# A graph-attention kernel: the selection matrix of layers 0 and 1 made on ScalarE instead of VectorE

## What is computed

```
h   = (x @ W).reshape(N_NODES, HEADS, HEAD_DIM)          # 6250, 8, 32
el, er = sums of h * al and of h * ar over HEAD_DIM
e   = leaky_relu(el[src] + er[dst], 0.2)
ex  = exp(e - m[dst]);  a = ex / segment_sum(ex, dst)[dst]
out = segment_sum(h[src] * a, dst)                       # then bias, leaky_relu in layers 0 and 1
```

## Time and profile before

| | us |
|---|---|
| median of 3 runs | 7243.95 |
| lowest, highest | 7237.48, 7246.24 |
| the profiled execution's own time | 7240.56 |
| its span | 7238.9 |
| mean granted TensorE clock | 0.901 of full speed |

### The profile page before, as it was taken

One profiled execution on the slowest core, in us unless ns is written; L12 is line 12 of the kernel. 1 busy time (PEld: TensorE's weight loads), 2 busy tenths in 40 slices (PEclk: granted clock), 3 DMA queues, 4 the chain that ended last, 5 costly groups with the idle time before them and its releaser, 6 DMA issues.

```text
span 7238.9 us, 140830 instructions
## 1 busy us (share of the span) xinstructions
PE 5473.8 (76%) x35030; PEld 4419.5 (61%) x35031; DVE 4464.1 (62%) x9891; ACT 1582.9 (22%) x4669; POOL 4550.8 (63%) x4739
## 2 busy tenths in 40 slices
PE   4566677777776666666767665678888899999999
PEld 2445555565564454555555553456777778888888
DVE  5455566666665555666676765666666665655554
ACT  2000001111110000000000000013344444555554
POOL 0677777777765777777777757777655454444331
PEclk9788888888887788889898987789999999999999
DMA  4555555555544555555555444444433333222221
GB/s 168 175 142 146 146 148 149 150 152 148 144 140 116 142 142 145 144 144 146 147 148 144 139 118 135 140 133 129 118 110 104 93 95 87 83 84 80 73 73 41
DMA packets 386096, 916.18 MB, mean 127 GB/s; under 512 B 130561, under 2 KB 192777, under 8 KB 385930
## 3 DMA queue, kind: packets, MB, share of 16 engines
q0 software_dynamic: 227904, 681.63, 34.8%
q1 hardware_dynamic: 115530, 194.09, 7.9%
q10 hardware_dynamic: 42624, 40.02, 1.6%
HBM read 871.89 MB, written 43.49 MB: 126 GB/s over the span
## 4 chain that ended last, share of the span: by engine, by line
PE 28%; POOL 28%; issue 23%; DVE 8%; DVEq 7%; DMA 3%; ACTq 2%; ACT 2%; POOLq 1%; SPq 0%
POOL gat L411 27%; PE bank L1446 9%; PE bank L1373 9%; PE bank L1362 6%; DVEq L254 2%; DMA gat<-table,meta 2%; DVE msg L1116 2%; ACTq L254 1%; DVE selT L1088 1%; DVE sel L1124 1%; PE bank L1316 1%; DVE lg L1106 1%; ACT L501 1%; DVEq L1142 1%; DVEq L1107 0%
## 5 line engine op out<-in xcount | busy, mean ns | idle before, releaser
L411 POOL DMA_INDIRECT gat<-table,meta x4716 | 4537.5, 962 | 2538.3 <-issue 1366.3
L1446 PE MATMUL bank<-msg,sel 128*128 x10560 | 3174.8, 452 | 1347.2 <-DVE sel L1124 1330.3
L1446 PEld LDWEIGHTS bank<-msg,sel 128*128 128x128 f32 x10560 | 2183.5, 217 | 1810.8 <-issue 1436.9
L1116 DVE SCALAR_TENSOR_TENSOR msg<-bank,gat 128x1056 f32 x1320 | 1658.3, 1256 | 273.9 <-ACT bank L544 250.2
L544 ACT ACTIVATE bank<-lg 128x32 f32<-128x32 f32 x1320 | 262.8, 199 | 4620.5 <-DVE lg L1110 4485.3
L1124 DVE TENSOR_TENSOR sel<-iota_t,meta 128x512 f32<-128x512 f32 x1320 | 903.4, 684 | 93.9 <-PE bank L1446 90.1
L1106 DVE TENSOR_TENSOR lg<-gat,bank 128x64 f32<-128x64 f32 x880 | 193.3, 220 | 999.8 <-POOLq L418 759.3
L1373 PE MATMUL bank<-w,region 128*128 128x256 f32 x3136 | 758.5, 385 | 31.8 <-ACT region L501 31.6
L1362 PEld LDWEIGHTS bank<-xT,w 128*128 128x128 f32 x6272 | 750.5, 192 | 15.8
L1362 PE MATMUL bank<-xT,w 128*128 128x128 f32 x6272 | 759.6, 276 | 0.0
L1416 PEld LDWEIGHTS bank<-uvb,selT 128*128 128x128 bf16 x10584 | 391.3, 98 | 445.7 <-DVE selT L1088 252.8
(11 more groups left out here) (215 smaller groups left out, 2559.5 us busy)
## 6 DMA issues: line engine op xcount, KB each, us to landing
dstb<-dst_lists SPq DMA_DIRECT2D x297, 512.0 KB
gat<-table,meta POOLq DMA_INDIRECT x4716
table<-hrow ACTq DMA_DIRECT2D x98, 140.0 KB, 2.7
w<-in_W SPq DMA_DIRECT2D x2, 4096.0 KB
table<-hrow SPq DMA_DIRECT2D x49, 140.0 KB, 1.8
region<-xnT_d ACTq DMA_DIRECT2D x50, 128.0 KB
region<-qT_d ACTq DMA_DIRECT2D x50, 128.0 KB
res<-in_x SPq DMA_DIRECT2D x1, 6272.0 KB, 25.4
```

What stands on the lines that cost most here:

```text
L411: pool.indirect_dma_start(gat[:, r, c, :], None, table[l], bass.IndirectOffsetOnAxis(meta[:, m, c, 0:1].bitcast(U32), 0)).then_inc(s_done, 16)
L1116: dve_v.scalar_tensor_tensor(msg[:, bass.ds(n % 2, 1), :, :].rearrange("p a c (h d) -> p (a c) h d", h=H), ex_p.unsqueeze(3).to_broadcast( ...
L1446: last = pe.matmul(acc[:, 0:MSG], sel[:, c, :], msg[:, bass.ds(m % 2, 1), c, :].rearrange("p a m -> p (a m)"), start=opens and c == 0, sto ...
```

## The change

In layers 0 and 1 VectorE no longer makes `sel`. At the start of `logits` it subtracts the tile's base from the 512 destination numbers of the pass (`within`, 128x4, two buffers). ScalarE, behind its exponential of the pass, waits on `agg_done`, takes for each of the 4 blocks the absolute value of (bias - node number), drains, and turns the distances into 1 or 0 by max(0, 1 - distance); it reports on a semaphore of its own, `sel_ready`. VectorE's `messages` now signals `tile_first`, `slot_done` or `tile_last`, and TensorE waits on `sel_ready` ahead of those. `select` returns at once in these layers, and `iota_t` is written in layer 2 only. The rest of the diff merges some semaphores of the setup phase (`flags_ready`, `slots_ready` and their like into `step_ready` and `step_summed`), wait for wait; it is cut here.

```diff
+        within = sb("within", [P, 2, CH])
...
+        sel_ready = [sem(f"sel_ready{l}") for l in range(LAYERS - 1)]
...
                     act.wait_ge(logit_ready[l], n)
                     act.activation(ex_p, lg[:], ACT.Exp).then_inc(ex_ready[l], 1)
+                    if l + 1 < LAYERS:
+                        act.wait_ge(agg_done[l], n)
+                        for c in range(CH):
+                            act.activation(sel[:, c, :], iota, ACT.Abs,
+                                           bias=within[:, bass.ds(n % 2, 1), c:c + 1].rearrange("p a c -> p (a c)"), scale=-1.0)
+                        act.drain()
+                        act.activation(sel[:], sel[:], ACT.Relu, bias=ones[:, 0:1], scale=-1.0).then_inc(sel_ready[l], 1)
...
                 dve.sem_inc(agg_done[l], 1)
+                if l + 1 < LAYERS:
+                    dve.sem_inc(sel_ready[l], AHEAD)
...
+                    if l + 1 < LAYERS:
+                        dve_v.tensor_scalar(within[:, bass.ds(n % 2, 1), :].rearrange("p a c -> p (a c)"),
+                                            meta[:, bass.ds(g % LISTS, 1), :, 1:2].rearrange("p a c w -> p (a c w)"),
+                                            base[:, bass.ds(T, 1)], None, ALU.subtract)
                     dve.wait_ge(gathered[l], g)
...
-                    if opening:
+                    if opening and l + 1 == LAYERS:
                         dve_v.tensor_scalar(iota_t[:], iota, base[:, bass.ds(T, 1)], None, ALU.add)
...
-                def messages(g, n):
+                def messages(g, n, done):
...
-                    dve_v.scalar_tensor_tensor(
+                    product = dve_v.scalar_tensor_tensor(
...
+                    if l + 1 < LAYERS:
+                        product.then_inc(done, 1)
 
                 def select(g, n, done):
 
+                    if l + 1 < LAYERS:
+                        return
                     dve.wait_ge(agg_done[l], n)
...
                 def aggregate(m, opens=False, closes=False):
 
+                    if l + 1 < LAYERS:
+                        pe.wait_ge(sel_ready[l], m)
                     for c in range(CH):
```

More of the change, by code:

```diff
@@ L200, in build @@
         x_in, k_in, w_in, d_in, late_in, experts_in = map(sem, ("x_in", "k_in", "w_in", "d_in", "late_in", "experts_in"))
-        ext_ready, var_ready, std_ready, flags_ready, flagsT_ready, slots_ready, sums_ready, ctl_ready = map(
-            sem, ("ext_ready", "var_ready", "std_ready", "flags_ready", "flagsT_ready", "slots_ready", "sums_ready",
-                  "ctl_ready"))
+        ext_ready, var_ready, std_ready, ctl_ready = map(sem, ("ext_ready", "var_ready", "std_ready", "ctl_ready"))
+        step_ready, step_summed = sem("step_ready"), sem("step_summed")
         turn_taken = sem("turn_taken")
@@ L208, in build @@
         ctl_out, ctl_in, zeros_ready = sem("ctl_out"), sem("ctl_in"), sem("zeros_ready")
[L209 removed]
+        d16_ready, d16_out = sem("d16_ready"), sem("d16_out")
         xn_ready, xn_free, xT_psum, xT_ready = map(sem, ("xn_ready", "xn_free", "xT_psum", "xT_ready"))
@@ L716, in _ @@
                 dve.drain()
-            dve.sem_inc(flags_ready, 1)
-            dve.wait_ge(flagsT_ready, 1)
+            dve.sem_inc(step_ready, 1)
+            dve.wait_ge(step_summed, 1)
             lf = small[:, 240:244]
@@ L748, in _ @@
             dve.drain()
-            dve_v.tensor_tensor(end, low, held, ALU.add).then_inc(ranges_ready, 1)
-            dve.wait_ge(prev_ready, 1)
+            dve_v.tensor_tensor(end, low, held, ALU.add).then_inc(step_ready, 1)
+            dve.wait_ge(step_summed, 2)
             dve_v.tensor_scalar(rows, low, 1.0, None, ALU.add)
@@ L754, in _ @@
             dve.drain()
-            dve_v.tensor_tensor(rows, held, share, ALU.subtract).then_inc(slots_ready, 1)
-            dve.wait_ge(sums_ready, 1)
+            dve_v.tensor_tensor(rows, held, share, ALU.subtract).then_inc(step_ready, 1)
+            dve.wait_ge(step_summed, 3)
             out_ctl = ismall[0:NT, 16:16 + CTL]
@@ L1162, in pairs @@
                     logits(T, first, n_first, first + 1, T, True)
-                    messages(first, n_first)
+                    messages(first, n_first, tile_first[l])
                     if l + 1 < LAYERS:
@@ L1186, in pairs @@
                             logits(T, g, n, g + 1, T)
-                            messages(g, n)
+                            messages(g, n, slot_done[l])
                             select(g, n, slot_done[l])
@@ L1191, in pairs @@
                     logits(T, last, n_last, g_next, T + 1)
-                    messages(last, n_last)
+                    messages(last, n_last, tile_last[l])
                     select(last, n_last, tile_last[l])
@@ L1281, in _ @@
             pe.wait_ge(k_in, 16)
-            pe.wait_ge(flags_ready, 1)
+            pe.wait_ge(step_ready, 1)
             fl = small[:, 128:128 + 2 * NT].rearrange("p (w t) -> p w t", w=2)
             pe.matmul(tp[0:NT, 0:P], fl[:, 0, :], ident, start=True, stop=True)
[L1286 to L1290, removed]
+            pe.matmul(tp[0:NT, P:2 * P], fl[:, 1, :], ident, start=True, stop=True).then_inc(step_summed, 1)
+            pe.wait_ge(step_ready, 2)
+            pe.matmul(tp[0:NT, 258:259], kc[0:NT, K_PREV:K_PREV + NT], small[0:NT, 238:239], start=True, stop=True).then_inc(step_summed, 1)
+            pe.wait_ge(step_ready, 3)
             held = small[0:NT, 239:242]
@@ L1293, in _ @@
             pe.matmul(tp[0:NT, 263:266], ones[0:NT, 0:NT], held, start=True, stop=True)
-            pe.matmul(tp[0:NT, 266:269], kc[0:NT, K_NEXT:K_NEXT + NT], held, start=True, stop=True).then_inc(sums_ready, 1)
+            pe.matmul(tp[0:NT, 266:269], kc[0:NT, K_NEXT:K_NEXT + NT], held, start=True, stop=True).then_inc(step_summed, 1)
             pe.wait_ge(ctl_ready, 1)
```

## The result

The changed kernel takes 8038.4 us (median of 4 runs, 8031.3 to 8061.5) against 7245.1 before: 793 us more, a ratio of 1.1106 (95% interval 1.1093 to 1.112). The forecast was 7510 with a range to 7720: slower was right, by about a third of the size.

What follows compares the result with a forecast made beforehand. GpSimd's gathers bound the kernel until the loop through `sel`, at 4.83 us a pass, takes over: +167 us, or +369 with a slower clock. The middle, +268, on 7240.6 gives 7508.6, stated as 7510; range 7180 to 7720.

Steps and rivals of the forecast that it cites:

- GpSimd set the pace: Layers 0 and 1 before the change: gathers cost 5.0 us a slot; only 117 us of stalls could be won.
- a ring through the one buffer of `sel`: Layers 0 and 1: products, hand-over, selection, hand-over; 3.58 us a pass before the change on average, binding nothing.
- the ring takes over at a stretch near 2.13 us: Between a pass's products and the next: below 2.13 us GpSimd stays the bound, 7124 to 7180 us; chance 0.17.
- layer 2 at zero: Layer 2 keeps its code, so its time was to change by 0.
- Abs needs no table load: ScalarE's selection: the opposing rival had two table loads of 1.28 us in each pass, some 9660 us; chance 0.02.
- the sum of the ring: Layers 0 and 1: 2.51 us of products plus 2.32 outside them, 4.83 us a pass, +167 us at an unchanged clock.
- The clock: TensorE's products in layers 0 and 1: up to 2.74 instead of 2.51 us a pass, 202 us more at most.
- the second rival: TensorE's products in layers 0 and 1: the slow clock stays on, 7800 us at 50% slow passes; chance 0.12.
- ScalarE's work between the hand-overs: ScalarE's selection each pass: four Abs 1.16 us, drain 0.08, Relu 0.70, together 1.94 us.
- The hand-over to TensorE: From the end of the selection to the first product: 0.19 us as before, the second wait costing nothing.
- The rest: Seams between tiles and ScalarE's copies per tile: seam gap 2.32 us instead of 4.6, copies adding nothing.
- what queues behind the new wait: Behind ScalarE's wait on agg_done: exponential, messages and copies per tile all fit into the ring, nothing added.

Runs made afterwards that it cites:

- r4_warm: Changed kernel plus 10 products of zeros a pass ahead of TensorE's wait on sel_ready, layer 1 only: 7766.9 us against 8045.2 for the changed kernel.
- r1_apart: Changed kernel with the four Abs writing to a buffer of their own, only the Relu waiting on agg_done: 7364.6 us against 7240.7 before, ratio 1.0171.
- the dose: Changed kernel with fewer of the four Abs per pass, output wrong: 7728.5 us with three, 7212.2 us with one.
- u2_three_abs: Changed kernel with three of the four Abs, block 3 of the selection left out: 7728.5 us, ratio 1.0673 to the kernel before.
- r3_dve_split: Changed kernel with the selection back on VectorE, separate waits, earlier slot_done and within kept: 7310.6 us against 7240.7 before, ratio 1.0093.
- u3_one_abs: Changed kernel with one of the four Abs, blocks 1 to 3 of the selection left out: 7212.2 us, ratio 0.996 to the kernel before.
- e4_wait_last: Changed kernel with an edit meant to move TensorE's sel_ready wait behind the messages' wait, order in fact unchanged; slow chip: 9946 against 9495 us, ratio 1.048.
- s4_wait_last: Repeat of the changed kernel with the edit to TensorE's wait order, which left the order unchanged; slow chip: 9835 against 9368 us, ratio 1.0498.
- e3_dve_split: Changed kernel with the selection back on VectorE and separate waits kept, on a slow chip: 9689 us against 9495 before, ratio 1.020.
- e1_apart: Changed kernel with the Abs in a buffer of their own, only the Relu waiting on agg_done, on a slow chip: 9837 us against 9495, ratio 1.036.

## Why the prediction was wrong

**Right.** The reading that GpSimd set the pace and that a ring through the one buffer of `sel` lay just beneath it; that ScalarE's idle time is no argument; that the ring takes over at a stretch near 2.13 us (1.67 is below the bend, 2.26 above); layer 2 at zero; Abs needs no table load: the changed kernel has 189 and 190 of them, as many as before. The trace agrees with the Trainium skill ("ScalarE: Activation LUTs", section on table sets), by which Abs is in every set.

**The terms that failed**, all in the sum of the ring, against 797 us measured where I had 268:
- *The clock*, taken at +101 us with 202 as the upper value. It was 337. I priced it by a stretch of the old trace (2.74 us of products), in which the ring wasn't the bound. r4_warm shows the mechanism: it is the second rival, which had 50% of the products at the slow clock at 7800 us; measured are (2.89 - 2.04)/(3.88 - 2.04) = 46%, and with the longer stretch that makes 8038. A rival with 0.12 should have had the larger part.
- *ScalarE's work between the hand-overs*, taken at 1.94 us. It is 2.07: four Abs are 1.28 and not 1.16 us, since one starts each (1.28 - 0.39)/3 = 0.30 us and the Gelu row's 0.26 did not carry over; the Relu is 0.72, not 0.70. That is 0.13 x 880 = 114 us. By the figures of the Trainium skill ("ScalarE: Activation LUTs", section on what ACT_TABLE_LOAD costs), which I set aside for that row, the estimates were 1.27 and 0.71, and the trace agrees with them. (They come to 0.12 us more than mine, or 106 us, and not the 97 of the prediction.) The row was of another function and read from PSUM; which of the two makes its spacing shorter was not tried.
- *The hand-over to TensorE*, taken at 0.19 us from the ring of before, with "TensorE's second wait costs nothing of its own". It is 0.30, and by the table above the second wait is the difference: 0.11 x 880 = 97 us. The first pass of every tile of the kernel before has two waits and 0.30 us, in the earlier trace rows from 613.55 to 613.85. With the term above, 2.56 instead of 2.32 us: 211 us.
- *The rest*, taken as no more than the stretch itself. The mean outside the products is 2.66, 0.10 over the stretch: 88 us. The seams are 3.23 us in layer 0 and 2.80 in layer 1 on average (4.21 and 2.95 before) and not 2.32: over the 2.56, 44 us. Another 29 us come from a copy that the prediction had at nothing ("so nothing is added"). Once a tile of layer 1 ScalarE's copy at L612 stands ahead of its exponential and its selection and waits for TensorE, whose work for it comes behind the products; the stretch is then 3.2 us, here 4407.39 to 4410.60:

```profile
4403.93 3.46 PE L1466 MATMUL bank<-msg,sel 128*128 x8 [2.27 <-ACT sel L552]
...
4407.85 0.38 ACT L612 ACTIVATE region<-bank 128x256 f32<-128x256 f32 x1 [4.22 <-PE bank L1341]
...
4410.60 3.31 PE L1466 MATMUL bank<-msg,sel 128*128 x8 [2.50 <-ACT sel L552]
```

One of the longest seams of the changed kernel (7 of the 48 in layer 0 are like it), 4.5 us from 2574.89 to 2579.38:

```profile
2571.83 0.72 ACT L552 ACTIVATE sel<-sel,kc 128x512 f32<-128x512 f32 x1
...
2572.73 0.19 DVE L1124 TENSOR_TENSOR lg<-lg 128x32 f32<-128x32 f32 x1
2572.85 2.04 PE L1466 MATMUL bank<-msg,sel 128*128 x8 [2.27 <-ACT sel L552]
...
2575.11 0.20 ACT L545 ACTIVATE bank<-lg 128x32 f32<-128x32 f32 x1 [2.56 <-issue]
...
2579.38 3.88 PE L1466 MATMUL bank<-msg,sel 128*128 x8 [3.54 <-DVE xn L1155]
```

The logits are there at 2572.92 and ScalarE is free at 2572.55, but its exponential starts at 2575.11: it is idle for 2.56 us on "issue". At this place its program loads the tile's slot numbers into registers (`tile_slots` at the head of `pairs`). By the program, ScalarE reached that place early before, and now the selection of the last pass stands ahead of it. The messages, `divide` and the next products follow late. The waits of the exponential put down to "issue" are 134.9 us in layer 0 of the changed kernel and 2.1 before. This is a step that I didn't follow when I asked what queues behind the new wait. That the register loads fill the 2.56 us is read from the program, and no run tried it.

From the forecast's 268: + 236 (clock) + 211 (stretch) + 88 (the rest) = 803, against 797. Most of these are places of the measured time. Shown by a run of their own are the clock's part (r4_warm) and the length of the stretch (r1_apart and the dose). u2_three_abs tests the step by itself: at 2.26 us, shorter than my 2.32, the time is 487 us over before and not 268.

No complete version tried beats the kernel before: r1_apart is the best with ScalarE's selection, 1.7% behind, and r3_dve_split is 0.9% behind; u3_one_abs is faster but leaves three quarters of the Abs out.

## What to carry to other kernels

Where one buffer passes between two engines, add up the whole ring (work, hand-overs, work) and compare it with the pace of the bound before moving a part of it to an idle engine: how busy that engine is says nothing. If TensorE is in the ring, price the products at both clocks, since a longer wait costs twice. Count the waits in a row ahead of the engine that takes the buffer as well: the second one was 0.11 us a pass here. Work can stay on the slower engine if only its last instruction has to wait for the buffer: an intermediate in a buffer of its own took 681 of 805 us away.

## What the runs showed of the hardware

- Products of zeros in TensorE's idle time raised the granted clock of the layer from 0.74 to 0.97 and shortened it by 266 us, although they delayed the products at the seams.
- The hand-over of the selection to TensorE was 0.19 us with one wait ahead of the product and 0.30 with two in a row, from VectorE as from ScalarE; the mechanism is open.
- Activations of one shape don't all repeat at the same rate: the Gelu from PSUM started 0.26 us apart, the Abs from SBUF 0.30.
- The same kernel took 7240 us on some chips and 9360 to 9500 on three others. There the excess of 11% shrank to 5% (e4_wait_last and s4_wait_last, whose order of waits is that of the changed kernel), while the small ones of 0.9 and 1.7% grew to 2.0 and 3.6% (e3_dve_split, e1_apart). What differs on these chips is open.
